# A vision block with a state-space scan and routed experts: the order of work between the scan and the experts

## The reference

```python
h = patches @ proj_w.T + proj_b + pos_emb
h = h + mamba(layernorm(h))      # projections, a causal convolution of 4 taps, silu; softplus step;
                                 # state = exp(A*dt)*state + dt*B*h over 64 steps, 384 channels x 16 states;
                                 # y = (C . state + D*h) * silu(gate); output projection
x = layernorm(h)
scores = softmax(x @ gate_w.T)   # 8 experts; the two largest per token, their weights normalised to sum 1
y = sum over the two experts e of weight * (silu(x @ w1[e].T) * (x @ w3[e].T)) @ w2[e].T
y = y + (silu(x @ ws1.T) * (x @ ws3.T)) @ ws2.T       # the shared expert, for every token
return h + y
```

## Time and profile before

| | us |
|---|---|
| median of 3 runs | 425.6 (425.19 to 426.79) |
| the profiled execution | 425.67 |
| its span | 423.7 |
| TensorE busy | 368.8 (87%) |
| VectorE busy | 224.3 (53%) |
| ScalarE busy | 214.4 (51%) |
| GpSimd busy | 211.9 (50%) |

### The profile page before, as it was taken

The page is one execution under the profiler, slowest core; times in us unless marked ns, Lnnn a source line. Parts: engine busy times, 40 slices in busy tenths (PEclk is TensorE's granted clock), DMA queues, the critical chain, the costliest instruction groups (busy, mean ns, idle before and its releaser), DMA issues.

```text
span 423.7 us, 5569 instructions
## 1 busy us (share of the span) xinstructions
PE 368.8 (87%) x1686; PEld 263.3 (62%) x1687; DVE 224.3 (53%) x329; ACT 214.4 (51%) x388; POOL 211.9 (50%) x159
## 2 busy tenths in 40 slices
PE   4789779899985999999999868956899999999980
PEld 4733235455553654667668767845688888888870
DVE  0577849665892775769881618836143223232310
ACT  0044889736797695694455545851233233323320
POOL 2110659974797475789998102750013344334433
PEclk9999959999998899999998967987899999999995
DMA  7940620000023152000299940323113222322221
GB/s 213 307 146 0 293 107 0 3 3 0 2 100 130 70 198 74 2 22 29 89 276 271 254 116 23 120 98 48 36 36 63 47 43 43 58 50 43 31 28 19
DMA packets 28691, 36.95 MB, mean 87 GB/s; under 512 B 6160, under 2 KB 24128, under 8 KB 27648
## 3 DMA queue, kind: packets, MB, share of 16 engines
q1 hardware_dynamic: 18864, 27.38, 21.5%
q0 software_dynamic: 4080, 4.39, 6.8%
q10 hardware_dynamic: 5728, 4.93, 4.1%
HBM read 28.29 MB, written 8.40 MB: 87 GB/s over the span
## 4 chain that ended last, share of the span: by engine, by line
PE 40%; ACT 18%; DMA 18%; issue 9%; DVE 7%; ACTq 5%; POOLq 1%; another core or an unknown queue 1%; SPq 0%; DVEq 0%
DMA out<-ysb,token_r 17%; PE ps L1321 12%; ACT decays L704 6%; PE ps L1338 6%; ACT diagB L692 5%; PE ps L1474 2%; PE ps L1233 2%; PE ps L1231 2%; DVE w L348 2%; ACTq L641 2%; DVE ysb L1142 1%; PE ps L1263 1%; PE ps L1439 1%; PE ps L1242 1%
## 5 line engine op out<-in xcount | busy, mean ns | idle before, releaser
L956 DVE TENSOR_TENSOR_SCAN states<-decays,ps 128x1024 f32<-128x1024 f32 x48 | 109.1, 2282 | 45.4 <-PE ps L1321 35.7
L516 POOL TENSOR_TENSOR states<-states,c_all 128x1024 f32<-128x1024 f32 x48 | 114.3, 2387 | 36.9 <-DVE states L956 36.3
L1321 PE MATMUL ps<-diagB,dt_uT 128*128 128x512 f32 x192 | 95.2, 621 | 1.5 <-ACT dt_uT L682 1.0
L594 POOL DMA_INDIRECT out<-ysb,token_r x23 | 36.1, 1571 | 67.4 <-DVE ysb L1142 50.4
L704 ACT ACTIVATE decays<-dt_uT,negA 128x504 f32<-128x504 f32 x96 | 60.3, 704 | 18.4 <-DVE states L956 18.4
L1338 PEld LDWEIGHTS ps<-ident,states 128*128 128x128 f32 x384 | 46.5, 145 | 23.0 <-issue 22.8
L1321 PEld LDWEIGHTS ps<-diagB,dt_uT 128*128 128x128 f32 x192 | 34.3, 198 | 32.7 <-issue 28.2
L1130 DVE TENSOR_TENSOR hm<-ps,sa 128x512 f32<-128x512 f32 x31 | 21.4, 690 | 60.1 <-PE ps L1445 56.3
L1474 PE MATMUL ps<-w,hT 128*128 (+1 forms) x248 | 46.8, 334 | 5.3 <-ACT hT L809 5.3
L1338 PE MATMUL ps<-ident,states 128*128 128x128 f32 x384 | 51.3, 278 | 0.0
L805 ACT ACTIVATE sa<-ps 128x512 f32<-128x512 f32 x31 | 18.6, 598 | 63.3 <-PE ps L1445 61.4
(11 more groups left out here) (174 smaller groups left out, 516.5 us busy)
## 6 DMA issues: line engine op xcount, KB each, us to landing
c_all<-c_scratch SPq DMA_DIRECT2D x8, 1024.0 KB, 4.8
w_raw<-in_w13T SPq DMA_DIRECT2D x9, 512.0 KB, 9.6
w_raw<-in_w13T SPq DMA_DIRECT2D x18, 256.0 KB, 9.0
w<-in_w2T SPq DMA_DIRECT2D x9, 384.0 KB, 9.1
xs<-rows_scratch SPq DMA_DIRECT2D x23, 128.0 KB, 2.4
rows_scratch<-dt_uT ACTq DMA_DIRECT2D x5, 520.0 KB, 8.6
c_all<-in_xT SPq DMA_DIRECT2D x4, 256.0 KB, 7.0
c_all<-in_xT SPq DMA_DIRECT2D x1, 1024.0 KB, 12.9
```

The lines of the kernel that those rows point to most:

```text
L516: pool.tensor_tensor(states[:, n % SLOTS, :], states[:, n % SLOTS, :], c_all[:, s, :], ALU.mult).then_inc(cs_ok, 1)
L594: pool.indirect_dma_start(out=out_d, out_offset=bass.IndirectOffsetOnAxis(ap=token_r[:, r:r + 1], axis=0), in_=ysb[:, r, :], in_offset=Non ...
L956: dve.tensor_tensor_scan(states[:, n % SLOTS, :], decays[:, n // PAIRS % DBUF, n % PAIRS, :, :, :].rearrange("p q n s -> p (q n s)"), unit ...
L1321: last = pe.matmul(unit_banks(n)[:, q, :], uT[:, g, i, 128 * t:128 * (t + 1)], diagB[:, s, q, :, :].rearrange("p n t -> p (n t)"), start=T ...
```

## The change

It touches only the stretch between the scan's end and the first slot tile.

- TensorE sums unit 47 directly after unit 46, then one filler (the first chunks of an output pair), unit 48, the skip product and the transposes back. The first group's logits and the other fillers come behind.
- The last group's transposes are done by pairs of tiles, each pair into one bank (4 and 7) with both halves of its columns. ScalarE copies pair 0, VectorE pair 1 (`tail_x`). The copy of the last 64 columns is made once for each pair. Logits of the last group start when pair 0 is copied. The first group's logits go to bank 5.
- Results of shared tiles are added in place into `h0`, with no buffer and no wait. SyncE stores them in two DMAs, of six tiles and of two, behind the scatters and the first loads of slot tiles.
- ScalarE loads the silu table and makes high part 5 ahead of the first x_high; x_high of tiles 0 and 1 come before the copies of the transposes, and the low halves wait for these. High part 9 comes before the exp. Low part 5 is made on VectorE ahead of the normalising, before high part 9; low part 6 goes to GpSimd.
- The token weights leave out the division by the sum of all exponents: (sum x 1e-20 + e1 + e2) replaces the sum of the normalised scores, six operations instead of eight. They come after the slots and give the signal to GpSimd.
- One step more is in the loop (`FIRST_STEP` 1 instead of 2), so tile 2's up product, hidden transposes of tile 1 and the down product of tile 0 come out of the hand-written part; `tile_experts` stays with step 2.

The diff, cut to its core:

```diff
-            first = BY_POOL + 1 + 2 * (s - FIRST_STEP)          # low_at
+            first = BY_POOL + 2 + 2 * (s - FIRST_STEP)
+        def pair_x_bank(p):
+            return FBANK if p else 4
+        def pair_x(p):
+            return (xnT[:, :, GT + 256 * p:GT + 256 * (p + 1)],
+                    ps[:, pair_x_bank(p), :].rearrange("p (k n) -> p k n", k=2))
-        FIRST_STEP, CONVERTED = 2, 10
+        FIRST_STEP, CONVERTED = 1, 10
# SyncE
+            def store_shared(first, end):
+                sp.wait_ge(ysb_ok, end)
+                sp.dma_start(sum_v[first:end].rearrange("s p d -> p s d"), h0[:, first:end, :]).then_inc(y_st, 16)
+            EARLY = TT - 2
-            for n in range(EARLY):
-                store_shared(n)
             sp.wait_ge(scat_st, 16 * 2 * TT)
             for n in range(2):
                 load_rows(n, n)
             sp.dma_start(info...)
-            for n in range(EARLY, TT - 1):
-                store_shared(n)
-            for n in range(2, 4):
+            store_shared(0, EARLY)
+            load_rows(2, 0)
+            store_shared(EARLY, TT)
+            for n in range(3, 5):
                 load_rows(n, n % 2)
-            store_shared(TT - 1)
-            load_rows(4, 0)
# GpSimd, after the deviation of group 1
+            pool.wait_ge(xn_ok, TPG * (G + 2))
+            low_part(pool, BY_POOL + 1)
+            pool.wait_ge(low_ok, BY_POOL + 2)
-            for r in range(2):
-                pool.wait_ge(y_st[r], 16 * TT // 2)
+            pool.wait_ge(y_st, 16 * 2)
# ScalarE
             for v in (3, 4):
                 high_part(act, v)
-            transposed_to_sbuf(act, G)
+            act.preload_act_table_set("silu_and_others")
+            high_part(act, 5)
...
+            act.wait_ge(xn_tr, G + 1)
             x_high(0, 0)
             x_high(1, 1)
-            act.preload_act_table_set("silu_and_others")
-            for v in (5, 6):
-                high_part(act, v)
+            transposed_to_sbuf(act, G)
+            high_part(act, 6)
             act.wait_ge(dbu_mm, UNITS)
             y_transposed(G * IC - 1)
-            high_part(act, 7)
+            for v in (7, 8):
+                high_part(act, v)
             silu(0, 0)
-            high_part(act, 8)
-            x_high(2, 0)
-            silu(1, 1)
+            act.wait_ge(xn_tr, G + 2)
+            out, x = pair_x(0)
+            act.activation(out, x, ACT.Copy).then_inc(tail_x[0], 1)
             high_part(act, 9)
-            h_copy(0, 0)
-            transposed_to_sbuf(act, G + 1)
-            x_high(3, 1)
             act.preload_act_table_set("natural_log_exp_and_others")
             act.wait_ge(lmax_ok, 1)
             act.activation(sc[:, :, :], lg[:, :, :], ACT.Exp).then_inc(lexp_ok, 1)
-            silu(2, 0)
-            h_copy(1, 1)
+            x_high(2, 0)
+            silu(1, 1)
+            act.wait_ge(tail_x[1], 1)
+            h_copy(0, 0)
# VectorE
+                    if n >= G and t % 2:                                   # in normed
+                        dve.wait_ge(xn_ok, TPG * n + t % TPG + 1)
+                        dve.tensor_copy(xn[:, t - 1:t + 1, D:2 * DA], xn[:, t - 1:t + 1, DA:D]).then_inc(ends_ok, 1)
-                    wait(dve, y_st[r], 16 * (s // 2))                      # in result, shared tiles
-                    dve.tensor_tensor(ysb[:, r, :], ps[:, 6 + r, 0:D], h0[:, s, :], ALU.add).then_inc(ysb_ok, 1)
+                    dve.tensor_tensor(h0[:, s, :], ps[:, 6 + r, 0:D], h0[:, s, :], ALU.add).then_inc(ysb_ok, 1)
-            read_logits(0)
             dve.wait_ge(cs_ok, UNITS - 1)
-            dve.wait_ge(x_high_ok, 2)
+            dve.wait_ge(xnT_ok, 2 * (G + 1))
             x_low(0, 0)
             x_low(1, 1)
+            gated_sum(G * IC - 1)
+            second_rows()
+            low_part(dve, BY_POOL)
+            normed(G + 1)
+            dve.wait_ge(xn_tr, G + 3)
+            out, x = pair_x(1)
+            dve.tensor_copy(out, x).then_inc(tail_x[1], 1)
+            read_logits(0)
             largest(0)
             largest_at(0)
-            gated_sum(G * IC - 1)
-            second_rows()
-            gated(0, 0)
-            x_low(2, 0)
-            normed(G + 1)
-            dve.wait_ge(xn_tr, G + 2)
-            dve.tensor_copy(xnT[:, 1, GT:T], ps[:, FBANK, :]).then_inc(xnT_ok, 1)
-            gated(1, 1)
-            low_part(dve, BY_POOL)
             read_logits(1)
             largest(1)
             largest_at(1)
             shifted_logits()
             one_hots()
-            token_weights()
+            gated(0, 0)
             tile_counts()
             slots()
-            x_low(3, 1)
-            result(0, 0)
-            gated(2, 0)
+            token_weights()
+            x_low(2, 0)
+            gated(1, 1)
# TensorE
+            def last_transposes(p):
+                out = ps[:, pair_x_bank(p), :].rearrange("p (k q n) -> p k q n", k=2, q=2)
+                for q in range(2):
+                    t = TPG + 2 * p + q
+                    pe.wait_ge(xn_ok, G * TPG + t + 1)
+                    pe.transpose(out[:, 0, q, :], xn[:, t, 0:DA], ident[:, :])
+                pe.wait_ge(ends_ok, p + 2)
+                for q in range(2):
+                    last = pe.transpose(out[:, 1, q, :], xn[:, TPG + 2 * p + q, DA:2 * DA], ident[:, :])
+                last.then_inc(xn_tr, 1)
             transposes(G)
             summed(UNITS - 3)
-            logits(0)
+            summed(UNITS - 2)
             pair_output(0, range(IC - 1))
-            summed(UNITS - 2)
-            pair_output(1, range(IC - 1))
-            skip(G * IC - 1)
             summed(UNITS - 1)
+            skip(G * IC - 1)
             sum_after_skip(G * IC - 1)
+            pair_output(1, range(IC - 1))
+            for p in range(2):
+                pair_output(p, range(IC - 1, IC))
             pe.wait_ge(ld_w2s, 16)
             pe.wait_ge(low_ok, IN_SCAN)
             up_first(0, 0, shared)
+            logits(0)
             for p in range(2):
-                pair_output(p, range(IC - 1, IC))
+                last_transposes(p)
+            logits(1)
             up_second(0, 0, shared)
             pe.wait_ge(h1_ok, TPG + 2)
-            up(1, 1)
+            up_first(1, 1, shared)
+            ranks()
+            up_second(1, 1, shared)
+            pe.wait_ge(lg_ok, 1)
             h_transposes(0, 0)
-            transposes(G + 1)
-            down(0, 0)
-            logits(1)
-            up_first(2, 0, shared)
-            h_transposes(1, 1)
-            ranks()
-            up_second(2, 0, shared)
```

More of the change, by code:

```diff
@@ L212, in program @@
         ends_ok = sem("ends_ok")
+        tail_x = [sem(f"tail_x{p}") for p in range(2)]
         xn_tr = sem("xn_tr")
@@ L275, in program @@
         ysb_ok = sem("ysb_ok")
-        y_st = [sem(f"y_st{r}") for r in range(2)]
+        y_st = sem("y_st")
         info_ld = sem("info_ld")
@@ L1112, in slot_weights @@
                 dve.wait_ge(slots_ok, 1)
-                for r in range(2):
-                    dve.wait_ge(y_st[r], 16 * TT // 2)
             def x_low(s, r):
@@ L1145, in between @@
             def between(s):
-                if s == FIRST_STEP + 1:
+                if s == 2:
                     tile_experts()
@@ L1188, in transposes @@
                 g = n % G
-                if n < G:
-                    banks, end = (2, 3), DB
-                else:
-                    banks, end = (4 if n > G else YBANK, FBANK), 128
+                banks, end = ((2, 3), DB) if n < G else ((YBANK, FBANK), 128)
                 if n == 1:
@@ L1469, in down @@
                 pe.wait_ge(hT_ok, s + 1)
-                if isinstance(s, int) and s == 1:
-                    pe.wait_ge(xnT_ok, 2 * (G + 2))
                 wait(pe, ysb_ok, s - 1)
```

51 lines of the change are left out of this document (21 added, 30 removed).

## The result

The changed kernel takes 408.02 us (median of 4 runs, 407.08 to 408.69). The kernel before takes 426.2 (4 runs, 425.19 to 427.11). The ratio is 0.9571, 95% interval 0.9543 to 0.9599. Forecast were 405 and a range of 399 to 417. Executions over 1.5% above the fastest of their kernel (a slower state, at a lower clock) are left out of all medians, ranges and ratios here. The profiled execution took 407.58 us, its span is 405.5, and its mean granted clock 0.961 (before: 0.936).

A forecast was written before the change was run, and what follows sets the result against it. The prediction took TensorE as the bound, with a dent in the tail from scan end to first expert tile. Gains 23.6 + 1.25, less 3 and 1.5, gave 20.35 off 425.67: 405.3, said as 405; range 399 to 417.

The forecast's parts named there:

- A: Tail after the scan, last sums first: the deviation would be there at 233.4, 6.5 us earlier.
- rival 2: ScalarE's queue still gates pair 0's copy because weight 6, 7 or 8 lands late: 410, at worst 415; chance 0.09.
- B: Last transposes by pairs, ScalarE block gone: last logits read at 238.1 instead of 254.41, 9.8 us of it from here.
- C: Routing, from reading the last logits to the token weights: weights at 245.7, slot numbers 15.8 us earlier.
- D: From routing to the first expert tile, by rows and by TensorE: up(8) at 274.2, 23.6 us earlier.
- F: What comes back in the tail: 3 us of idle time without releaser, 1.5 us of slow clock (bounds 0 and 6.8).
- E: Behind the first expert tile, up(8) to up(12): 19.5 us instead of 20.75, a gain of 1.25.
- Rival 3: TensorE's clock stays at the lower level through the shared tiles, making the kernel slower: 428; chance 0.03.
- Rival 4: Better than forecast, with neither idle time nor slow clock: 400.8; chance 0.06.

The follow-up runs named there:

- old stores: Changed kernel with shared-tile results again through two buffers and single small stores, as before: 407.99 us, ratio 0.9693.
- weights first: Changed kernel with the token weights moved ahead of the counts: 407.02 us, ratio 0.9656.
- all three: Changed kernel with token weights before counts, second up half before the last transposes, and load of rows 3 ahead of the second store: 403.27 us, ratio 0.9479.
- logits split: Changed kernel with the three edits, plus the first group's logits in two halves around the second up half: 402.88 us, ratio 0.9463.
- third group: Last set of experiments: three repairs together, sums with low part 5, low parts copied by one input, first logits halved; kernel before had a median of 425.1 us.
- one-input low parts: Changed kernel with VectorE's low parts from the seventh on replaced by a one-input copy, subtraction left out: 416.01 us (one run).

## Why the prediction was right, and where not

The direction, the range and the chain of steps held: 407.58 measured in the profile, 405.3 forecast for it. The 2.3 us between them are several terms that partly cancel, so that the forecast came this close is in part luck: it took off 3 us for idle time that didn't come, and had the clock at 1.5 us where it cost 5.0. The last scan ended 1.28 us earlier than in the profile before (222.08 and 220.80), ahead of everything that was changed, so 1.28 is added to each time of the changed kernel before it is held against a step.

**A held with 1.1 us less.** The deviation was to be there at 233.4 and came at 233.20 + 1.28 = 234.5. The tie of low parts and moments came as foreseen (230.72 and 230.79). The step failed in what follows it: 1.15 + 1.01 us and their gaps, 2.4 together, where I left 1.5. The first of the two takes 0.20 us in the kernel before. Here it starts at 230.95, inside low part 5, which the change had put there (230.82 to 232.04), and ends at 232.10, just behind it. In every kernel with both the early sums and the moved low part one of the two operations is longer like that (1.15 instead of 0.20, or 1.86 instead of 1.01), and in none of the others. So the moved low part, which the sum had as free, costs 0.9 us on this path. The weights landed late, as rival 2 had it (2.04 us of wait at ScalarE), and it cost little, since the copy of y came at 224.85.

**B held in kind: the block of 5.14 us is gone and returned nowhere.** The last logits were read at 239.96 + 1.28 = 241.2 instead of 238.1. 1.1 of that is A, and 1.6 is the clock: the last logits took 4.2 us, not 2.6. The rest is 0.4 at their start. That the moved low part alone carries 7.0 us and the early sums alone nothing was not separated in the sum, where A had 6.5 and B 9.8. By the traces A's 6.5 become worth something only by what stands in B: a queue in which nothing of the shared tiles is ahead of the normalising and the transposes.

**C was 1.4 us short.** The token weights were to be there at 245.7 and came at 249.01 + 1.28 = 250.3, after 9.05 us instead of 7.6. The step "TensorE does two up halves, then the ranks" took 4.8 us for the halves at half clock, not 2.9, and VectorE waited 1.77 us for it. The token weights on the path cost 1.2, as said, and ahead of the counts they are hidden (tail 1.0 shorter).

**D held in its result, with both paths later.** Scatters: 24.66 us instead of 21.33, which the prediction carried over from before. That is the step of D that failed. VectorE's low parts lie beside the scatters in both kernels (eight before, ten now), and in both a scatter that starts inside one ends 0.83 us or more behind it: 251.50 + 1.89 = 253.39 is 0.85 after the end of the low parts at 249.98 + 2.56, and 257.56 + 1.97 is 0.84 after 257.47 + 1.22. In the kernel before 263.40 + 1.33 is 0.85 after 262.66 + 1.22:

```profile
263.40 1.33 POOL L582 DMA_INDIRECT rows_scratch<-xn,pos_i  x1 [0.30 <-issue]
...
262.66 1.22 DVE L348 TENSOR_TENSOR w<-w_raw,w 128x1024 fp32r<-128x1024 f32 x1
```

What differs is where in a low part a scatter happens to start. In the kernel before none starts in the first 0.6 us of one, and the longest takes 1.37 us; here four start within the first 0.2 us and take 1.89 to 2.03. The Trainium skill, "GPSIMD Engine Reference", section "1. Specifications", says that GpSimd shares its SBUF interfaces with VectorE, with contention from VectorE instructions in a 2-port performance mode or with two SBUF inputs; the runs agree for those with two SBUF inputs, for a software DMA (up to 1.07 us more) as well as for arithmetic (0.95 more in A), and no row says in which mode the low parts by one input ran. In the second execution of the changed kernel and in four variants (old stores, weights first, all three, logits split) the chain that ended last runs through the scatters, so their length bounds those. Here, from the last scatter's end to rows in use it took 3.89 us (1.70 to the issue and 2.2 for the load), the 3.9 of the prediction. TensorE: up(2) 4.5 us later than forecast (250.7 and 246.15), up(7) 7.4 later. Its five steps took 6.07, 5.54, 4.50, 5.60 and 4.51 instead of 23.35 together: 1.6 for the clock, and two steps with idle time of the kind issue (0.73 and 0.81) where I had one. Then 4.77 to the first expert tile, the 4.7 of the forecast, with no low part ahead of it. So up(8) was at 280.39 + 1.28 = 281.7, against 274.2 + 4.5 of F = 278.7.

**E: 19.83 instead of 19.5.** The step with the wait for rows 3 took 5.69, 1.0 above the others, where 0.7 was taken.

**F: both terms wrong, in opposite ways.** The idle time without a releaser was 0, not 3. It isn't a property of the changed kernel: the kernel before has none either in a second execution, and two variants in the third group have it. The clock cost 1.6 + 1.8 + 1.6 = 5.0 us, not 1.5, inside the bound of 6.8. The last 1.6 belongs to this execution: in the second one the clock is 1.00 from 250 to 256, after the same 2.35 us of idle time, and its tail is 79.2 all the same, because there the rows came last. The prediction weighed a rule on idle gaps, by which the clock would have cost 0. It fell behind runs of 8-column products, in eight traces with no idle time over 0.3 us near, so idle gaps alone were the wrong thing to count.

The 7.5 us at up(8) without F are 1.1 (A), 5.0 (clock), 1.3 (start steps) and 0.1. F had 4.5 of them, which leaves 3.0; with E's 0.3, 0.1 each behind the tail and around the span, and 1.3 of early scan taken off, that is 2.2 of the 2.3.

What the change is worth depends on the kernel before: 18 us beside its runs at 426, 14.0 beside those at 421.4. Where both had no idle time without a releaser, the ratio is 0.967 and the tail 13.0 us shorter (92.2 and 79.2): 7.0 by low part 5 (tried alone) and 0.3 by the early sums on top of it (tried together), and as the rest, which was not taken apart, 5.7 by the pairs, by the transposes ahead of the up products and by the order behind them, of which the new stores take up to 1 back. The other 4.3 us of the profiled difference are the idle time without a releaser in the kernel before; its 15 runs beside the result and in the third group took 423.49 us or more, the 27 of the other two groups 423.45 or less. Rival 3, a slow clock through the shared tiles, did not come: after 254.3 it is at 1.00. Rival 4's 400.8 was out of reach by the clock.

**Open.** What VectorE and ScalarE wait for in the idle time without a releaser. It was there only in profiles whose neighbouring runs of the kernel before took 425 us or more (the kernel before, sums and low part 5, one-input low parts), and not in all of those; in none where they took 421. The three groups of experiments ran on three chips, so the chip may be what matters; that was not tried apart. It comes while scatters are under way, with the old stores and with the new. Whether single-input operations make it longer was not tried apart, nor whether they hold a scatter when it starts early in one. That splitting the bunch of small products keeps the clock up rests on one pair of kernels, and why the same bunch brought no fall behind the last logits in two kernels (low part 5 alone, and sums with it) is not shown.

## What to carry to other kernels

Ahead of a critical product, look at what each engine's queue has in front of it: one low part moved within VectorE's queue was worth 7.0 us, and sums made 4.9 us earlier were worth 0.3 as long as work of another stage stood between them and their use. A moved operation also acts on its new neighbours: low part 5 cost GpSimd 0.9 us where it came to lie. Give durations carried over from the kernel before a margin where they depend on when another engine's operation starts: the scatters grew from 21.3 to 24.7 us beside the same kind of low parts. Run and profile the kernel before in each group of runs, since the kernel before took 4 us more in two groups than in two others.

## What the runs showed of the hardware

A software DMA's issue on GpSimd takes 0.96 us by itself (the first of the sixteen 1.25). When it starts in a VectorE operation that reads two SBUF tensors, it ends 0.83 us or more after that one, in all traces but for two scatters that start within 0.04 us of its start and take 0.96. It takes 1.0 us when it starts near the end of a low part of 1.22 us, and 1.9 to 2.0 when it starts in the first 0.2 us. In a gated product with one input from PSUM it takes 0.96 (at 253.69). TensorE's granted clock fell from 1.00 to 0.54 (between its two levels, 2.4 and 1.2 GHz) in the microsecond from 233 on while it was busy without a gap, and stayed at 0.97 in 230 to 240 when the small products were split by six products of 512 columns. In all thirteen traces with the first group's logits in one piece it fell within 3 us of their end, but behind the last group's logits in the kernel with sums and low part 5 it stayed at 1.00 (240 to 260). The same program has executions with 5 us of idle time for which the profile names no releaser, and others with none.
